# Other instruction orders on four engines in the last network of a two-layer adapter FFN kernel, with one more gate slot and one more up slot

## What is computed

```
def _L1_ffn_ref(x, gate_q, gate_s, up_q, up_s, down_q, down_s):   # H = 512, I = 1792, G = 128
    def dequant(q, s, g=G):
        O, In = q.shape
        return (q.reshape(O, In // g, g).astype(s.dtype) * s[:, :, None]).reshape(O, In)
    Wg = dequant(gate_q, gate_s)
    Wu = dequant(up_q, up_s)
    Wd = dequant(down_q, down_s)
    gate_score = jax.nn.silu(jnp.einsum('bsh,ih->bsi', x, Wg))
    intermediate = gate_score * jnp.einsum('bsh,ih->bsi', x, Wu)
    return jnp.einsum('bsi,hi->bsh', intermediate, Wd)
x = x + _L0_ffn_ref(_L0_cond_ref(x, ...), ...)
x = x + _L1_ffn_ref(_L1_cond_ref(x, ...), ...)
```

## Time and profile before

| | us |
|---|---|
| median of 3 runs | 677.3 (676.59 to 677.47) |
| profiled execution, its own time | 677.13 |
| its span (first to last instruction) | 675.5 |
| last network, part 1: units 0 to 6 | from 499.56 |
| part 1: down phase | from 555.39 |
| part 2: units 7 to 13 | from 582.42 |
| part 2: down phase | from 637.53 |

### The profile page before, as it was taken

How to read it: one execution, slowest core, us unless ns; L and a number is a source line. 1 busy time by engine, 2 the same in 40 slices (tenths; PEclk the granted TensorE clock), 3 DMA queues, 4 the chain that set the end, 5 groups by cost and what they waited for, 6 DMA issues and landing times.

```text
span 675.5 us, 8095 instructions
## 1 busy us (share of the span) xinstructions
PE 651.4 (96%) x2952; PEld 533.0 (79%) x2952; DVE 410.1 (61%) x478; ACT 306.6 (45%) x394; POOL 160.6 (24%) x130
## 2 busy tenths in 40 slices
PE   8979999999999999999999999999999999999993
PEld 6868888888788888888888888888877777877772
DVE  5875674444556444444353443443668888988895
ACT  5785725245543232232322222321557776477741
POOL 4640020000000400000000000000005776877766
PEclk9979999999999999999999999999999999999997
DMA  8510022101011212310101110120132111211102
GB/s 242 158 59 24 24 86 77 62 5 39 18 39 63 85 40 93 121 54 28 62 32 62 31 58 28 41 36 31 48 101 86 56 54 63 94 63 56 55 32 93
DMA packets 22470, 42.23 MB, mean 63 GB/s; under 512 B 9524, under 2 KB 10548, under 8 KB 22388
## 3 DMA queue, kind: packets, MB, share of 16 engines
q1 hardware_dynamic: 20388, 38.56, 18.1%
q0 software_dynamic: 2048, 3.22, 1.8%
HBM read 39.67 MB, written 2.10 MB: 62 GB/s over the span
## 4 chain that ended last, share of the span: by engine, by line
PE 83%; ACT 6%; DVE 5%; issue 3%; SPq 2%; DMA 1%; POOL 0%; POOLq 0%; DVEq 0%; ACTq 0%
PE ps_up L1198 7%; PE ps_up L1199 7%; PE ps_up L1200 7%; PE ps_down L1198 7%; PE ps_down L1199 7%; PE ps_down L1200 7%; PE ps_gate L1198 7%; PE ps_gate L1199 6%; PE ps_gate L1200 6%; PE ps_gate L1312 3%; PE ps_gate L1313 2%; PE ps_up L1312 2%; PE ps_m L1234 2%; PE ps_m L1312 2%; PE ps_up L1313 2%
## 5 line engine op out<-in xcount | busy, mean ns | idle before, releaser
L570 POOL TENSOR_TENSOR up_sum<-up_sum,up_more 128x1024 f32<-128x1024 f32 x14 | 33.8, 2416 | 271.9 <-DVE up_more L987 271.9
L699 ACT ACTIVATE act_hi<-gated 128x512 fp32r<-128x512 f32 (+2 forms) x50 | 31.5, 632 | 122.4 <-DVE gated L971 122.4
L1198 PE MATMUL ps_up<-h_hi,w_hi 128*128 128x512 f32 (+1 forms) x208 | 81.3, 391 | 0.2 <-DVE w_lo L882 0.2
L1199 PE MATMUL ps_up<-h_lo,w_hi 128*128 128x512 f32 (+1 forms) x208 | 81.2, 390 | 0.0
L1200 PE MATMUL ps_up<-h_hi,w_lo 128*128 128x512 f32 (+1 forms) x208 | 81.0, 389 | 0.0
L971 DVE TENSOR_TENSOR gated<-gated,ps_up 128x512 f32<-128x512 f32 (+1 forms) x48 | 32.9, 687 | 76.5 <-PE ps_up L1200 53.8
L1198 PE MATMUL ps_gate<-h_hi,w_hi 128*128 128x512 f32 (+1 forms) x192 | 77.0, 401 | 1.4 <-DVE h_lo L882 0.9
L631 ACT ACTIVATE w_hi<-w_raw 128x1024 fp32r<-128x1024 f32 (+4 forms) x44 | 41.8, 950 | 80.2 <-DVE w_raw L889 63.3
L1199 PE MATMUL ps_gate<-h_lo,w_hi 128*128 128x512 f32 (+1 forms) x192 | 75.7, 394 | 0.0
L1200 PE MATMUL ps_gate<-h_hi,w_lo 128*128 128x512 f32 (+1 forms) x192 | 75.6, 394 | 0.0
L1198 PE MATMUL ps_down<-act_hi,w_hi 128*128 128x512 f32 (+1 forms) x180 | 70.7, 393 | 0.0
(11 more groups left out here) (187 smaller groups left out, 1367.3 us busy)
## 6 DMA issues: line engine op xcount, KB each, us to landing
w_raw<-in_ffn_gu SPq DMA_DIRECT2D x14, 512.0 KB, 3.5
w_int<-in_ffn_gu SPq DMA_DIRECT2D x14, 512.0 KB, 3.5
w_raw<-in_cond_gu SPq DMA_DIRECT2D x9, 512.0 KB, 3.5
w_raw<-in_ffn_dn SPq DMA_DIRECT2D x8, 448.0 KB, 3.1
w_int<-in_ffn_dn SPq DMA_DIRECT2D x8, 448.0 KB, 3.1
xp<-in_x SPq DMA_DIRECT2D x8, 256.0 KB, 5.1
xp<-in_x SPq DMA_DIRECT2D x1, 2048.0 KB, 10.4
out_t<-xp SPq DMA_DIRECT2D x8, 256.0 KB, 2.0
```

The costliest lines, as they stand in the source:

```text
L570: nc.gpsimd.tensor_tensor(up_sum[:, u % 2, :], up_sum[:, u % 2, :], up_more[:, u % 2, :], ALU.add).then_inc(up_done, 1)
L699: nc.scalar.activation(act_hi[0:m, ds(2 * i + jj, 1), chunk(c)].rearrange("p a n -> p (a n)"), gated[0:m, c, :], ACT.Copy).then_inc(act_hi ...
L1198: nc.tensor.matmul(ps[0:m, :], w_hi[0:r, s, cols], rhs_hi(k, r), start=start and n == 0, stop=False)
L1199: nc.tensor.matmul(ps[0:m, :], w_hi[0:r, s, cols], rhs_lo(k, r), start=False, stop=False)
```

## The change

Nothing is added or removed; the same instructions stand in other orders, and two buffers get one more slot. In `plan_groups` group g2 changes places with u1, and in the down phase slice 5 of tiles 0 and 1 comes after slices 0 to 4 of both. gate_sum has four slots and up_sum three; up_more and down_last move to the room of the earlier phases' weights.

```
-    gate_up = [("g", 0, "a"), ("g", 1, "v"), ("u", 0, "a"), ("u", 1, "v"), ("g", 2, "v"), ("u", 2, "a"), ("u", 3, "v"), ("g", 3, "v")]
+    gate_up = [("g", 0, "a"), ("g", 1, "v"), ("u", 0, "a"), ("g", 2, "v"), ("u", 1, "v"), ("u", 2, "a"), ("u", 3, "v"), ("g", 3, "v")]
-        for o, ks in ((0, range(6)), (1, range(6)), (0, (6,)), (1, (6,)), (2, range(7)), (3, range(7))):
+        for o, ks in ((0, range(5)), (1, range(5)), (0, (5,)), (1, (5,)), (0, (6,)), (1, (6,)), (2, range(7)), (3, range(7))):
...
-        gate_sum = place("gate_sum", [P, 3, TOK], F32, at["h"])
-        up_sum = place("up_sum", [P, 2, TOK], F32, at["h"] + 12 * KB)
-        up_more = place("up_more", [P, 2, TOK], F32, at["h"] + 20 * KB)
-        down_last = place("down_last", [P, TOK], F32, at["h"] + 12 * KB)
+        gate_sum = place("gate_sum", [P, 4, TOK], F32, at["h"])
+        up_sum = place("up_sum", [P, 3, TOK], F32, at["h"] + 16 * KB)
+        up_more = place("up_more", [P, 2, TOK], F32, at["w"])
+        down_last = place("down_last", [P, TOK], F32, at["w"] + 8 * KB)
...
 (GpSimd, for each unit)
                     unit_join(u)
                     unit_product(u)
-                    unit_lo(u)
+                    if j > 0:
+                        unit_lo(u - 1)
+                unit_lo(ACT_TILES * (part + 1) - 1)
...
 (ScalarE)
             def group_tile(n, u, begun):
+                if u > 3:
+                    act.wait_ge(unit_ready, u - 3)
+                scaled(group_of[n, "g", 0], gate_sum[:, u % 4, :])
                 if u > 2:
-                    act.wait_ge(unit_ready, u - 2)
-                scaled(group_of[n, "g", 0], gate_sum[:, u % 3, :])
+                    for c in range(CH):
+                        act.wait_ge(half_done[c], u - 2)
+                scaled(group_of[n, "u", 0], up_sum[:, u % 3, :])
                 if begun:
                     unit_silu(u - 1)
+                integers(n + 2)
                 if u > 1:
-                    for c in range(CH):
-                        act.wait_ge(half_done[c], u - 1)
-                scaled(group_of[n, "u", 0], up_sum[:, u % 2, :])
-                integers(n + 2)
+                    act.wait_ge(up_done, u - 1)
                 scaled(group_of[n, "u", 2], up_more[:, u % 2, :])
                 if begun:
                     unit_hi(u - 1)
             def group_down(n, part, o):
...
                 scaled(group_of[n, "d", 0], down_sum[:, m % 3, :])
+                if o == 1:
+                    unit_hi(last)
+                scaled(group_of[n, "d", 2], down_more[m % 3][:, :])
                 if o == 0:
-                    unit_silu(ACT_TILES * (part + 1) - 1)
-                scaled(group_of[n, "d", 2], down_more[m % 3][:, :])
+                    unit_silu(last)
                 if n + 2 < 2 * (ACT_TILES + HK):
                     integers(n + 2)
-                if o == 0:
-                    unit_hi(ACT_TILES * (part + 1) - 1)
```

On VectorE the add of g2 moves ahead of that of u1, so the product of the unit before comes after three adds instead of two:

```
                 added(group_of[n, "g", 1], gate).then_inc(dve_read, 1)
+                dve.wait_ge(dve_read, group_of[n, "g", 1].ev)
+                added(group_of[n, "g", 2], gate).then_inc(dve_read, 1)
                 dve.wait_ge(act_read, group_of[n, "u", 0].ea)
                 added(group_of[n, "u", 1], up).then_inc(dve_read, 1)
                 if begun:
                     unit_product(u - 1)
-                dve.wait_ge(dve_read, group_of[n, "g", 1].ev)
-                added(group_of[n, "g", 2], gate).then_inc(dve_read, 1)
```

More of the change, by code:

```diff
@@ L569, in unit_join @@
                 pool.wait_ge(dve_read, group_of[part * (ACT_TILES + HK) + j, "u", 3].ev)
-                nc.gpsimd.tensor_tensor(up_sum[:, u % 2, :], up_sum[:, u % 2, :], up_more[:, u % 2, :], ALU.add).then_inc(up_done, 1)
+                nc.gpsimd.tensor_tensor(up_sum[:, u % 3, :], up_sum[:, u % 3, :], up_more[:, u % 2, :], ALU.add).then_inc(up_done, 1)
             def unit_product(u):
@@ L574, in unit_product @@
                 pool.wait_ge(up_done, u + 1)
-                gate = gate_sum[:, u % 3, chunk(1)]
-                nc.gpsimd.tensor_tensor(gate, gate, up_sum[:, u % 2, chunk(1)], ALU.mult).then_inc(half_done[1], 1)
+                gate = gate_sum[:, u % 4, chunk(1)]
+                nc.gpsimd.tensor_tensor(gate, gate, up_sum[:, u % 3, chunk(1)], ALU.mult).then_inc(half_done[1], 1)
             def unit_lo(u):
@@ L580, in unit_lo @@
                 j = u % ACT_TILES
[L581 removed]
+                nc.gpsimd.tensor_tensor(act_lo[:, j, :], gate_sum[:, u % 4, :], act_hi[:, j, :].bitcast(F32), ALU.subtract).then_inc(unit_ready, 1)
             def down_sums(part, o):
@@ L704, in unit_silu @@
                 act.wait_ge(dve_read, group_of[part * (ACT_TILES + HK) + j, "g", 3].ev)
-                nc.scalar.activation(gate_sum[:, u % 3, :], gate_sum[:, u % 3, :], ACT.Silu).then_inc(gate_done, 1)
+                nc.scalar.activation(gate_sum[:, u % 4, :], gate_sum[:, u % 4, :], ACT.Silu).then_inc(gate_done, 1)
             def unit_hi(u):
@@ L709, in unit_hi @@
                     act.wait_ge(half_done[c], u + 1)
-                nc.scalar.activation(act_hi[:, u % ACT_TILES, :], gate_sum[:, u % 3, :], ACT.Copy).then_inc(unit_hi_done, 1)
+                nc.scalar.activation(act_hi[:, u % ACT_TILES, :], gate_sum[:, u % 4, :], ACT.Copy).then_inc(unit_hi_done, 1)
             def scaled(g, out_):
@@ L731, in group_down @@
             def group_down(n, part, o):
-                m = HK * part + o
+                m, last = HK * part + o, ACT_TILES * (part + 1) - 1
                 if m > 2:
@@ L993, in unit_product @@
                 dve.wait_ge(up_done, u + 1)
-                gate = gate_sum[:, u % 3, chunk(0)]
-                nc.vector.tensor_tensor(gate, gate, up_sum[:, u % 2, chunk(0)], ALU.mult).then_inc(half_done[0], 1)
+                gate = gate_sum[:, u % 4, chunk(0)]
+                nc.vector.tensor_tensor(gate, gate, up_sum[:, u % 3, chunk(0)], ALU.mult).then_inc(half_done[0], 1)
             def group_tile(n, u, begun):
-                gate, up, more = gate_sum[:, u % 3, :], up_sum[:, u % 2, :], up_more[:, u % 2, :]
+                gate, up, more = gate_sum[:, u % 4, :], up_sum[:, u % 3, :], up_more[:, u % 2, :]
                 dve.wait_ge(act_read, group_of[n, "g", 0].ea)
                 added(group_of[n, "g", 1], gate).then_inc(dve_read, 1)
+                dve.wait_ge(dve_read, group_of[n, "g", 1].ev)
+                added(group_of[n, "g", 2], gate).then_inc(dve_read, 1)
                 dve.wait_ge(act_read, group_of[n, "u", 0].ea)
@@ L1020, in group_down, with group_down_more @@
                 added(group_of[n, "d", 3], more).then_inc(dve_read, 1)
+                if o == 0:
+                    unit_product(ACT_TILES * (part + 1) - 1)
                 dve.wait_ge(dve_read, group_of[n, "d", 1].ev)
                 added(group_of[n, "d", 4], both).then_inc(dve_read, 1)
-                if o == 0:
-                    unit_product(ACT_TILES * (part + 1) - 1)
+            def group_down_more(n, part, o):
                 dve.wait_ge(dve_read, group_of[n, "d", 3].ev)
-                added(group_of[n, "d", 5], more).then_inc(dve_read, 1)
+                added(group_of[n, "d", 5], down_more[(HK * part + o) % 3][:, :]).then_inc(dve_read, 1)
             def group_down_end(n, part, o):
@@ L1181, in _ @@
                 for o in range(2):
+                    group_down_more(n + o, part, o)
+                for o in range(2):
                     group_down_end(n + o, part, o)
```

## The result

| | before | after |
|---|---|---|
| median, us | 677.3 (676.59 to 677.47) | 670.03 (668.6 to 670.44) |
| ratio, with its 95% interval | | 0.9891 (0.9874 to 0.9908) |
| profiled execution, its own time | 677.13 | 668.6 |
| its span | 675.5 | 667.0 |

The account below looks back on a forecast made before the run. The bound was a once-a-unit ring through GpSimd, VectorE and ScalarE, not TensorE. Gains 4.3 + 4.2 + 0.2 + 0.2 = 8.9 us took 677.13 to 668.2; the median, 0.2 above, was 668.4, range 667.2 to 684.6.

Parts of the forecast that it names:

- The ring: Last network's units: a once-a-unit chain through GpSimd, VectorE and ScalarE, 8.04 us, said to bound the kernel.
- third rival, the change does not reach the bound: Unit-start stall has another cause, such as ScalarE's g0, so the time stays at 677 us; chance 0.05.
- VectorE's and GpSimd's times in a unit: From a unit's first matmul: VectorE asks for its product at 6.22 us, GpSimd's lo starts at 6.31.
- The collision: In the units, VectorE's product asks about 0.1 us before GpSimd's queued lo and gets the port; no time lost.
- held in the units only: VectorE's product is held behind lo in the units but wins in the down phase: 684.5 us; chance 0.08.
- point of decision: In the units, whether VectorE's product or GpSimd's lo issues first decides who waits, at a lead of zero.
- The chance of 0.24: Chance that the changed kernel is slower: unit products held 0.08, all products held 0.16.
- the held state: In the units, lo holds VectorE's product and this repeats: 8.9 us a unit against 7.98.
- The down phases: First: d4's bank stalls 1.0 us, queue about 0.4 more; second: GpSimd's chain sets the end; gain 0.2 each.
- the main case: Whole kernel: VectorE's unit products win the port, median 668.4 us, own range 667.2 to 669.6; chance 0.65.
- products now and then lost to lo: Some unit products held behind GpSimd's lo but still faster, 669.6 to 675.9 us; chance 0.06.

Follow-up runs that it names:

- The split: Changed kernel with the product split at column 640, so VectorE takes 640 columns and GpSimd 384, instead of at 512: 684.08 us.
- one kernel with the same net: Changed kernel with GpSimd's lo also waiting for VectorE's half of the product: 669.66 us, ratio 0.9871.
- the repeat: The changed kernel run once more with no edit: 669.15 us, ratio 0.9871.
- silu first: Changed kernel with ScalarE's silu of a part's last unit ahead of d2 of tile 0 in the down phases: 669.24 us.

## Why the prediction was right

**The bound.** Right. The ring lo, join, product, VectorE's held product, hi, lo was summed to 8.04 us. That this sum meets the unit's time, which the prediction held against its third rival, proves little: it is the distance from one lo to the next (531.31 - 523.27) cut into pieces. What speaks for the ring in those rows is that each piece begins within 0.15 us of the end of the one before it, and what shows it is the run with lo put back. Putting lo back closes it at 7.93, with every other part of the change in place; cutting it leaves TensorE without a wait. The rival "the change does not reach the bound" is out.

**VectorE's and GpSimd's times in a unit.** Both sums were 0.07 to 0.09 us short, in the same direction, so the lead that hung on them held. With unit 3 beginning at 522.33, g2 is added at 3.90 (forecast 3.82), u1 at 5.10 (5.02), VectorE asks at 6.29 (6.22), GpSimd's product starts at 5.14 (5.05) and lo at 6.40 (6.31): a lead of 0.11 for a forecast of 0.09. In unit 2 the lead is smaller, 0.03, because GpSimd's product starts 0.08 earlier in that unit (520.14, the unit beginning at 515.08); it was enough.

**The collision.** The step that carried the most doubt was that VectorE, first by 0.1 us, gets the port against an instruction already queued on GpSimd. It did, in every unit of both traces of the changed kernel. Lo was said to begin 0.5 late; in the records it begins at once and lasts 0.45 to 0.53 longer.

**The rival "held in the units only".** It was given 684.5 us; the kernel that forces it took 684.08. Units 8.8 apart for a forecast of 8.9, TensorE's waits on ps_down for up_more as named, and 1.6 us for each held product (15.2 us of net, and 1.0 less at d4's bank, over ten). Its point of decision, a lead of zero, is bracketed: 0.03 us ahead wins; less than 0.1 behind loses at the end of the span (L1054 at 660.57, the second half of the L599 row from 659.27 beginning at 660.49), and so does 0.1 behind with three gate slots. The forecast was thus right by little. The split moved the lead by 0.28 us, from 0.11 and 0.03 ahead to 0.17 and 0.25 behind, and made the change slower than before; by the bracket about 0.2 would do. The chance of 0.24 for that was no false caution.

**The slots.** The prediction said that the fourth gate slot "only" lets ScalarE write early and that no wait is left on it. That holds of the changed kernel. It didn't say what the slot is worth: 13.6 us of net (180.8 against 167.2), because the wait that comes back without it ends in the held state.

**The down phases.** The mechanism was right, the size a little high: gains of 0.13 and 0.06 for a forecast of 0.2 each. These are DVE's row of the product in the first one and PE's row at d4's bank, where the earlier trace rows were:

```profile
556.61 1.63 DVE L999 TENSOR_TENSOR gate_sum<-gate_sum,up_sum 128x512 f32<-128x512 f32 x1
```

```profile
559.50 0.50 PE L1322 MATMUL ps_gate<-act_hi,w_q 128*128 128x512 f32 x1 [0.74 <-DVE down_sum L991]
```

VectorE asked at 5.3 and was held to 6.9, as forecast (556.61 to 558.24, the phase beginning at 551.34); the phase loses 1.5 us against 25.40 for a forecast of 1.4. In the second phase GpSimd's first join starts at 13.2, as forecast, its first sum at 15.71 for 15.6, and the chain behind is the same.

**The total.** The forecast was 668.2 for the profiled execution, which took 668.6: 0.26 of the 0.4 lie ahead of the last network. The median, 670.03, is 1.6 above the 668.4 that was given for it. It lies outside the range of 667.2 to 669.6 that was given for the main case, in one that was meant for products now and then lost to lo, and none was lost; only the range as a whole, which reaches to the slower side, holds it. The step that failed is the one from the profiled execution to the median: I took the median to lie 0.2 above the profiled execution, as before. Here the profiled execution was the lowest of its four. The nets of the two traces of the changed kernel agree to 0.1 us, and one kernel with the same net came to the last network 1.9 us later; the repeat's median is 669.15.

## What to carry to other kernels

Where a VectorE instruction that reads two operands from SBUF meets a GpSimd instruction, write down for each such pair which one asks first and by how much: the one that is late waits for the whole of the other, and a lead of a tenth of a us decides over a per cent of the time. Where moving an instruction opens such a race, look for what keeps the favoured engine early (here one more gate slot), or make the other one wait for it; in the units that wait cost nothing that could be measured (in the down phase with silu first it cost 0.3 us), and it stops one late arrival from being carried through all units behind it. A change whose parts do harm or little alone may still be right as a whole, so undo its parts one at a time from the full version rather than only adding them to the old one.

## What the runs showed of the hardware

- A VectorE product that is already waiting gets in between two GpSimd instructions that follow without a pause. In the down phase it is recorded at 556.61, waits behind GpSimd's product (556.40 to 557.69), and ends at 558.24; the two lo queued behind (5.20 us for both from 557.65) wait. The Trainium skill (SBUF — State Buffer, Who interferes with whom) has issue order decide; the trace agrees if a GpSimd instruction that is only queued behind another counts as not yet issued.
- A VectorE product of 512 columns that is held ends 0.54 to 0.56 us after the end of the GpSimd instruction that holds it, in all the traces; one of 640 columns ends 0.68 after it. It loses when it is recorded 0.1 us behind.
- The held state feeds itself. One add 0.36 us late put the changed kernel with the memset into it, and it stayed to the end of the part at 1.7 us a unit; with three gate slots it lasted for eight of ten units.
- A 128x256 memset on VectorE right ahead of the product let it win at 0.15 to 0.24 us behind lo, where without one it loses at 0.1, 0.17 and 0.25. Counted from the memset, the winners were recorded from 0.04 us ahead of lo to 0.05 behind it and the losers 0.21 to 0.35 behind. The memset took 0.27 us in both cases. Why it keeps lo off in the first and isn't held in the second was not settled.
- Three memsets of one column cost about 0.02 us together, too little to serve as a delay.
